# Gated linear attention: gate logits on four row strips of TensorE, scans by head between the tiles, the output gate projected early, and a per-token norm from 64 columns

## The reference, cut to what matters

```python
q = (x @ Wq).reshape(B, T, 4, 128);  k = (x @ Wk).reshape(B, T, 4, 128);  v = (x @ Wv).reshape(B, T, 4, 32)
gk = jax.nn.log_sigmoid(x @ Wgk1 @ Wgk2 + bgk2) / 16.0        # Wgk1 128x16, Wgk2 16x512: 4 heads x 128
# in chunks of 64 tokens: G = cumsum(gk) within the chunk
qg = q * exp(G) * scale;  k_intra = k * exp(-G);  kg = k * exp(G[last] - G)
o = tril(qg @ k_intra.T) @ v + qg @ S;   S = S * exp(G[last]) + kg.T @ v
g = (x @ Wg).reshape(B, T, 4, 32)
o = o * rsqrt(mean(o * o, axis=-1) + EPS) * gnw               # mean over the 32 values of a head
out = (o * silu(g)).reshape(B, T, 128) @ Wo
```

## Time and profile before

| | |
|---|---|
| median of 3 timed runs | 1602.13 us |
| lowest, highest | 1594.62, 1602.46 us |
| span of the profiled execution | 1577.7 us |
| from that span to the median of the runs | 24.4 us |
| busy in the span | PE 1150.9, DVE 839.3, ACT 752.6, POOL 533.3 us |

### The profile page before, as it was taken

How to read it: one execution, slowest core, us unless ns; L and a number is a source line. 1 busy time by engine, 2 the same in 40 slices (tenths; PEclk the granted TensorE clock), 3 DMA queues, 4 the chain that set the end, 5 groups by cost and what they waited for, 6 DMA issues and landing times. The chain is left out here.

```text
span 1577.7 us, 20354 instructions
## 1 busy us (share of the span) xinstructions
PE 1150.9 (73%) x6768; PEld 804.0 (51%) x6768; DVE 839.3 (53%) x1759; ACT 752.6 (48%) x1801; POOL 533.3 (34%) x532
## 2 busy tenths in 40 slices
PE   6639958996999676367686776876777748287897
PEld 2138825672666222255564555655555536174554
DVE  2075555534553566466665665656556546034536
ACT  4722336771875544255444454445445434074425
POOL 2000000000000448366666666666666653600000
PEclk8559978995999566576656767667666555578999
DMA  5000000000003235112222122222222212200000
GB/s 181 0 1 0 0 0 0 1 0 0 1 1 87 76 90 139 46 32 56 54 54 56 32 56 54 57 55 47 41 57 55 54 25 41 57 5 27 1 1 27
DMA packets 74367, 61.82 MB, mean 39 GB/s; under 512 B 31570, under 2 KB 58900, under 8 KB 73764
## 3 DMA queue, kind: packets, MB, share of 16 engines
q1 hardware_dynamic: 58404, 36.28, 9.3%
q0 software_dynamic: 15872, 24.41, 6.7%
HBM read 52.51 MB, written 8.13 MB: 38 GB/s over the span
## 5 line engine op out<-in xcount | busy, mean ns | idle before, releaser
L542 POOL DMA_INDIRECT arena_lo<-key_table,idx_T x496 | 491.9, 992 | 304.0 <-issue 134.8
L576 PE MATMUL bank<-arena_lo 128*32 128x32 f32 (+6 forms) x1656 | 208.5, 276 | 116.1 <-ACT arena_hi L1280 66.6
L576 PEld LDWEIGHTS bank<-arena_lo 128*32 128x32 f32 (+5 forms) x1656 | 177.7, 166 | 168.4 <-issue 131.2
L555 POOL TENSOR_TENSOR arena_lo<-arena_lo 128x512 f32<-128x512 f32 x8 | 11.8, 1474 | 516.4 <-DVE arena_lo L1608 516.1
L856 PE MATMUL bank<-ident,arena_hi 128*96 128x128 f32 x512 | 113.4, 363 | 24.4 <-DVE arena_hi L1700 23.2
L1254 ACT ACTIVATE arena_hi<-bank 96x512 f32<-96x512 f32 x128 | 74.7, 583 | 113.6 <-remote 67.3
L1280 ACT ACTIVATE arena_hi<-bank 32x128 f32<-32x128 f32 x128 | 33.5, 262 | 194.0 <-remote 160.7
L1668 DVE SCALAR_TENSOR_TENSOR arena_lo<-arena_lo,iw 128x512 f32<-128x512 f32 (+4 forms) x114 | 76.1, 668 | 81.5 <-ACT arena_lo L1237 46.2
L1237 ACT ACTIVATE arena_lo<-bank 128x512 f32<-128x512 f32 (+4 forms) x152 | 76.5, 512 | 65.7 <-remote 30.9
L576 PE MATMUL bank<-index_k_hi,index_q 128*128 128x512 f32 (+5 forms) x160 | 94.0, 589 | 18.7 <-issue 17.0
L1710 DVE CUSTOM_DVE_ANT_0 arena_hi<-bank,score_mask 128x208 f32<-128x208 f32 x124 | 46.4, 374 | 106.9 <-issue 71.0
(11 more groups left out here) (257 smaller groups left out, 2484.3 us busy)
## 6 DMA issues: line engine op xcount, KB each, us to landing
arena_lo<-key_table,idx_T POOLq DMA_INDIRECT x496
arena_lo<-q_l SPq DMA_DIRECT2D x64, 64.0 KB
arena_lo<-q_lat SPq DMA_DIRECT2D x32, 128.0 KB
arena_lo<-q_g SPq DMA_DIRECT2D x64, 64.0 KB
h<-in_h SPq DMA_DIRECT2D x2, 1024.0 KB, 8.2
q_l<-arena_hi SPq DMA_DIRECT2D x8, 256.0 KB
q_g<-arena_hi SPq DMA_DIRECT2D x8, 256.0 KB
q_lat<-arena_hi SPq DMA_DIRECT2D x8, 256.0 KB
```

Source lines behind the costliest of these rows:

```text
L542: pool.indirect_dma_start(out=G[b][:, q, :], out_offset=None, in_=key_table[0:index_width(i), :], in_offset=bass.IndirectOffsetOnAxis(ap=i ...
L576: return pe.matmul(out_, lhsT, rhs, start=start, stop=stop, **kw)
```

## The change

- The logits: `Wgk1` and `Wgk2` come from the host laid out anew. `Wgk1` is 128x128, its 16 columns repeated at the rows 0, 32, 64 and 96 of the product, the other columns zero; `Wgk2` is 128x128 with head `h`'s piece in the rows `32h` to `32h+15`. The four heads' matmuls then each use one strip of 32 rows of the array (`tile_position`) and a bank of their own. ACT does `Abs` alone; DVE reads the bank after it and writes the negated logit (`g_lin`). The next chunk's 16 values are projected and copied before this chunk's `Exp`.
- The sums: one head of one chunk at a time (`cumulate(k)`), rectifying in the same instruction as the addition. Five are done before the tiles, the other eleven one behind each of the tiles 0 to 10. ACT's `Exp` of a tile waits only for its own chunk.
- The output gate is projected into the banks 4 to 7 and taken through `Silu` before the first tile, into a buffer of its own (`gate`, named `arena_hi`).
- The tiles: the loops are written out. DVE no longer copies a tile of `xn` (`stage`, L1459); PE reads `xn` itself. ACT squares the tile's result out of `bank[3]` behind the tile, PE multiplies that 128x128 square with `head_mean` (128x4) to 4 columns of `bank[6]`, with the tokens on the partitions, and DVE's copy out of `bank[3]` becomes a product with `gnw` and the gate, behind ACT's square.
- The norm: ACT takes the root of the 128x64 columns, DVE the reciprocal, ACT spreads each column over 32 (`o_cols`), PE transposes them back to the layout of `oT`, DVE multiplies, PE projects with `gWo`, and DVE adds to `x`, chunk by chunk.
- Some buffers move, and `Wgk1`, `Wgk2` are 64 KB each in place of 8 and 32 KB; `mean_head` (64 KB) gives way to `head_mean` (2 KB).

```diff
-                with pe.Fori(0, NCH) as c:
+                def lowrank(c):
                     pe.wait_ge(ln_applied, LN0 + 4 * L_GLA + 1 + c)
-                    pe.wait_ge(g_rect, GH * c + 1)
-                    mm(bank[0][0:16, :], Wgk1[:], chunk(xn, c)).then_inc(g_r, 1)
+                    if c >= 1:
+                        pe.wait_ge(g_lin, GH * (c - 1) + 1)
+                    mm(bank[0], Wgk1[:], chunk(xn, c)).then_inc(g_r, 1)
+                def logits(c):
+                    strip = P // GH
                     pe.wait_ge(g_rs, c + 1)
                     for h in range(GH):
-                        pe.wait_ge(g_rect, GH * c + h + 1)
-                        mm(bank[h], Wgk2[:, h * GDK:(h + 1) * GDK], r_sb).then_inc(g_z, 1)
-                pe.wait_ge(g_rect, GH * NCH + GH)
+                        if c >= 1:
+                            pe.wait_ge(g_lin, GH * (c - 1) + h + 1)
+                        rows_ = slice(h * strip, (h + 1) * strip)
+                        mm(bank[h], Wgk2[rows_, :], r_sb[rows_, :], tile_position=(h * strip, 0)).then_inc(g_z, 1)
+                lowrank(0)
+                for c in range(NCH):
+                    logits(c)
+                    if c + 1 < NCH:
+                        lowrank(c + 1)
+                for c in range(NCH):
+                    mm(bank[4 + c], gWg[:], chunk(xn, c)).then_inc(g_gp, 1)
+                pe.wait_ge(g_lin, GH * NCH)
...
+                def mean_square(i):
+                    pe.wait_ge(g_osq, i + 1)
+                    mm(bank[6][:, 2 * P + GH * i:2 * P + GH * (i + 1)], o_sq, head_mean[:], skip_group_check=True)\
+                        .then_inc(g_oms, 1)
...
                     pe.wait_ge(g_S, 2 * i + 1)
+                    if not first:
+                        mean_square(i - 1)
...
                 project(0, "keys", first=True)
                 project(0, "queries", first=True)
+                pe.wait_ge(g_gate, NCH)
                 tile(0, 0, first=True)
-                with pe.Fori(0, NT // 2 - 1) as r:
-                    for u in (1, 0):
-                        tile(2 * r + 2 - u, u)
+                for i in range(1, NT - 1):
+                    tile(i, i % 2)
                 tile(NT - 1, 1, last_tile=True)
-                with pe.Fori(0, 2) as r:
-                    for u in range(2):
-                        c = 2 * r + u
-                        pe.wait_ge(g_gate, c + 1)
-                        mm(bank[u], gWg[:], chunk(xn, c)).then_inc(g_gp, 1)
-                with pe.Fori(0, 2) as r:
-                    for u in range(2):
-                        pe.wait_ge(g_osq, 2 * r + u + 1)
-                        mm(bank[2 + u], mean_head[:], o_sq[:, u, :]).then_inc(g_oms, 1)
-                    for u in range(2):
-                        pe.wait_ge(g_on, 2 * r + u + 1)
-                        mm(bank[u], gWo[:], chunk(oT, 2 * r + u)).then_inc(g_y, 1)
+                pe.wait_ge(g_S, 2 * NT + 1)
+                mean_square(NT - 1)
+                pe.wait_ge(g_qk, 2 * NT)
+                pe.wait_ge(g_vts, NT)
+                pe.wait_ge(g_out, NT)
+                pe.wait_ge(g_osq, NT)
+                def project_out(c):
+                    pe.wait_ge(g_on, c + 1)
+                    if c >= 2:
+                        pe.wait_ge(x_ready, 4 * L_FFN0 + c - 1)
+                    mm(bank[2 + c % 2], gWo[:], chunk(oT, c)).then_inc(g_y, 1)
+                for c in range(NCH):
+                    pe.wait_ge(g_oc, NCH + c + 1)
+                    if c >= 2:
+                        pe.wait_ge(g_on, c - 1)
+                    for j in range(C // P):
+                        last = pe.transpose(bank[c % 2][:, j * P:(j + 1) * P],
+                                            o_cols[c % 2][:, GH * j:GH * (j + 1), :].rearrange("p a b -> p (a b)"), ident[:])
+                    last.then_inc(g_ort, 1)
+                    if c >= 1:
+                        project_out(c - 1)
+                project_out(NCH - 1)
...
-                act.wait_ge(g_nb, 1)
+                def lowrank(c):
+                    act.wait_ge(g_r, c + 1)
+                    if c >= 1:
+                        act.wait_ge(g_z, GH * c)
+                    fn(r_sb, bank[0], ACT.Copy).then_inc(g_rs, 1)
+                lowrank(0)
                 for c in range(NCH):
-                    act.wait_ge(g_r, c + 1)
-                    fn(r_sb, bank[0][0:16, :], ACT.Copy).then_inc(g_rs, 1)
                     for h in range(GH):
                         act.wait_ge(g_z, GH * c + h + 1)
-                        fn(chunk(G_all[:, h, :], c), bank[h], ACT.Abs, bias=bgk2[:, h:h + 1])
-                        fn(chunk(relu_z[:, h, :], c), bank[h], ACT.Relu, scale=-1.0, bias=neg_bgk2[:, h:h + 1])\
-                            .then_inc(g_rect, 1)
-                    act.wait_ge(g_rect, GH * (c + 2))
+                        fn(chunk(G_all[:, h, :], c), bank[h], ACT.Abs, bias=bgk2[:, h:h + 1]).then_inc(g_rect, 1)
+                    if c + 1 < NCH:
+                        lowrank(c + 1)
+                    act.wait_ge(g_rect, GH * (c + 1))
                     g = G_all[:, :, bass.ds(c * C, C)]
                     steps.did(fn(g, g, ACT.Exp, scale=-1.0))
                 steps.leave(NCH, 1)
                 for c in range(NCH):
                     g = G_all[:, :, bass.ds(c * C, C)]
                     fn(g, g, ACT.Ln, bias=one_col).then_inc(g_ln, 1)
+                for c in range(NCH):
+                    act.wait_ge(g_gp, c + 1)
+                    fn(chunk(gate, c), bank[4 + c], ACT.Silu).then_inc(g_gate, 1)
 
                 def prepare(n, u, first=False):
 
                     if not first:
                         act.wait_ge(g_S, 2 * n - 1)
                         act.wait_ge(g_qk, 2 * n - 1)
-                    act.wait_ge(g_G, NT)
+                    act.wait_ge(g_G, GH * (n * P // C + 1))
...
+                def square(i):
+                    act.wait_ge(g_o, i + 1)
+                    if i >= 1:
+                        act.wait_ge(g_oms, i)
+                    fn(o_sq, bank[3][:, 0:P], ACT.Square).then_inc(g_osq, 1)
                 def tile(i, u, first=False, last_tile=False):
+                    if not first:
+                        square(i - 1)
...
+                square(NT - 1)
+                act.wait_ge(g_oms, NT)
+                fn(o_sd, bank[6][:, 2 * P:2 * P + NT * GH], ACT.Sqrt, bias=eps_col).then_inc(g_osd, 1)
+                act.wait_ge(g_osd, 2)
                 for c in range(NCH):
-                    act.wait_ge(g_gp, c + 1)
-                    fn(chunk(gate, c), bank[c % 2], ACT.Silu).then_inc(g_gate, 1)
-                act.wait_ge(g_out, NT)
-                with act.Fori(0, 2) as r:
-                    for u in range(2):
-                        fn(o_sq[:, u, :], chunk(oT, 2 * r + u), ACT.Square).then_inc(g_osq, 1)
-                    for u in range(2):
-                        act.wait_ge(g_oms, 2 * r + u + 1)
-                        fn(o_sd[:, u, :], bank[2 + u], ACT.Sqrt, bias=eps_col).then_inc(g_osd, 1)
+                    if c >= 2:
+                        act.wait_ge(g_ort, NCH + c - 1)
+                    per = GH * C // P
+                    fn(o_cols[c % 2], o_sd[:, per * c:per * (c + 1)].unsqueeze(2).to_broadcast([P, per, GDV]), ACT.Copy)\
+                        .then_inc(g_oc, 1)
...
-                with dve.Fori(0, NCH) as c:
-                    steps.enter(c, 1)
+                for c in range(NCH):
+                    for h in range(GH):
+                        dve.wait_ge(g_rect, GH * c + h + 1)
+                        if c == 0 and h == 0:
+                            dve.wait_ge(g_nb, 1)
+                        v.tensor_scalar(chunk(relu_z[:, h, :], c), bank[h], -1.0, neg_bgk2[:, h:h + 1], ALU.mult, ALU.add)\
+                            .then_inc(g_lin, 1)
+                def cumulate(k):
+                    c, h = k // GH, k % GH
                     dve.wait_ge(g_ln, c + 1)
-                    g, z = (a[:, :, bass.ds(c * C, C)] for a in (G_all, relu_z))
-                    steps.did(v.tensor_tensor(z, z, g, ALU.add))
-                    for h in range(GH):
-                        last = v.tensor_tensor_scan(chunk(G_all[:, h, :], c), scan_keep[:], chunk(relu_z[:, h, :], c),
-                                                    0.0, ALU.mult, ALU.add)
-                    last.then_inc(g_G, C // P)
-                steps.leave(1, NCH)
+                    dve.wait_ge(g_lin, k + 1)
+                    g, z = (chunk(a[:, h, :], c) for a in (G_all, relu_z))
+                    steps.did(v.scalar_tensor_tensor(z, z, 0.0, g, ALU.max, ALU.add))
+                    v.tensor_tensor_scan(g, scan_keep[:], z, 0.0, ALU.mult, ALU.add).then_inc(g_G, 1)
+                for k in range(GH + 1):
+                    cumulate(k)
...
                 def read_out(n):
-                    dve.wait_ge(g_o, n + 1)
```

(50 more changed lines are left out.)

49 lines of the change are left out of this document (26 added, 23 removed).

## The result

The changed kernel takes 1534.2 us (median of 4 runs, 1523.6 to 1544.0) against 1598.4 us before (4 runs, 1589.3 to 1602.5): a ratio of 0.962, 95% interval 0.954 to 0.969. Forecast were 1547 us, within 1534 to 1562. The profiled execution took 1542.15 us with a span of 1540.3. Some executions run slower as a whole at a lower granted clock: the medians in this text are over all executions, the ratios and intervals leave those out, so that a ratio can differ a little from the quotient of two medians.

A forecast was written before the change was run, and what follows sets the result against it. Engines were taken to wait on each other in turn, with PE bounding only the tiles. Gains 37.6 + 0 - 3.6 - 5.2 + 25.0 = 53.8, plus 1.2, made 55; 1602.1 - 55 = 1547 us, range 1534 to 1562.

The forecast's parts named there:

- Logits, 5.9 us a chunk, last Exp at 51.9: Logits stage: four heads side by side in 1.71 us, 5.9 us from Exp to Exp; gain 21.3 us.
- the strips' rival: Logits: strips don't run side by side, 6.8 us a chunk, 15 us lost, 1562 us; chance 0.08.
- that of the written order: Logits: passes start in written order, 4.3 us a chunk, 1552 us in all; chance 0.08.
- The 1.2 us added for the logits' clock: Logits: PE's clock perhaps up in part with four strips at work; 1.2 us more gain.
- First tile's Exp at 66.5: Between logits and tiles: ACT's Ln, Silu and table loads set the first Exp, 66.5 against 104.1; gain so far 37.6 us.
- First tile, even: First tile: projections already made but PE longer at half clock; 11.3 us from Exp to second tile as before, gain 0.
- Tiles, +8.8: Tiles: mean's matmul adds 0.24 us a tile, 3.6 in all; late scans add 1.74 us three times, 5.2.
- 2.63 us idle didn't lower the clock: Tiles: PE's earlier 2.63 us idle left the clock up, an argument against it falling at pauses of 1.74 us.
- The rival of the falling clock: Tiles: half clock makes each about 5.9 us longer, slower kernel from 10 tiles on, 1641 us with all 16; chance 0.02.
- Norm and output, 15.5 us: From the last tile's start to the next layer's first matmul: 15.5 us against 40.5; gain 25.0, bounds 20 and 26.3.
- The layer norm behind it, unchanged: Layer norm behind the output projection: left unchanged, no gain or loss counted.
- The median of the runs lies 24.4 above the span.: Whole kernel, from profiled span to run time: span 1577.7 us, median of the runs 1602.1 before the change.

The follow-up runs named there:

- the copy: after run again, unchanged; this time no GpSimd cast held up DVE's products in the first layer norm: 1372.7 us against 1423.7 before, ratio 0.966.
- after: The changed kernel as described, against the kernel before: 1534.2 us against 1598.4, ratio 0.962.
- its own experiment: The changed kernel with all four heads' logits weights on one strip of rows 0 to 31, one behind another: 1378.7 us, ratio 0.966 to before.
- the idle matmuls: The changed kernel with 14 matmuls that nobody reads on PE ahead of the first tile: 1553.8 us, ratio 0.967 to before.
- the other two groups: Unchanged repeats of before and after, each pair on one chip: 1423.7 and 1372.7 us, ratio 0.966; 1417.9 and 1360.4 us, ratio 0.960.

## Why the prediction was right, and where not

Set beside the copy of after without the collision (the forecast knew only a layer norm without it), the layer went from 222.6 to 170.3 us, and the stretch behind it from 28.7 to 26.3: 54.7 us, where 55 were forecast. With the collision on both sides (225.6 and 175.0, the stretch behind 29.5 and 27.7) it is 52.4. That the sum comes so near is in part luck: its terms missed in both directions, and two of the signs that the prediction itself named for being wrong did show. The clock was below 1.0 between the second tile and the last (0.95 over the 14 tiles), and tiles without a chunk's edge took over 6.6 us (7.39 and 6.98, the ones behind a long tile). Term by term:

- **Logits, 5.9 us a chunk, last Exp at 51.9.** The last Exp ended at 51.5 in the copy (58.0 in after, behind the collision), so the gain of 21.3 holds. But the period is 6.5: I let the Exp (1.91) cover the logits (1.71), and with 2.09 for them and 0.65 and 0.4 of hand-over they are what ACT waits for. The first chunk, at full clock (1.14 us for eight records), was earlier than I had it and made up for it. On the factor: 2.09 us against 7.19 is 3.4 times, between the 4 that I took and the 3.07 of the Trainium skill (TensorE: Matmul & The Clock Gate, Part 3), and the 2.2 us by that rule was the nearer. The two groups of four starts are as forecast: the strips' rival and that of the written order are refuted, the first by its own experiment. The 1.2 us added for the logits' clock has no row of its own: granted were 0.69 in the copy in place of 0.54, and the last Exp came 0.4 earlier than forecast.
- **First tile's Exp at 66.5.** 65.2 in the copy. ACT set it, as said; 1.84 us for a sum and scan, with 1.95 taken. The terms that the prediction names add up to 65.8, not 66.5 (51.9 and 1.28, 7.68, 1.28, 2.36, 1.28), so that 0.7 us of the miss is in the sum.
- **First tile, even.** 10.2 us in after against 11.26, 1.1 better, mostly at half clock (0.66 granted on the mean). What the full clock gives was shown by the idle matmuls: 2.3 us in one pair of profiles, 2.4 in the other.
- **Tiles, +8.8.** They cost 10.6 in after and 11.9 in the copy. The mean's matmul costs 0.12 a tile and not 0.24 (6.21 against 6.09), 1.7 us in all. The late scan costs 1.60 each, with 1.74 forecast, three times. The step that failed is the clock: "2.63 us idle didn't lower the clock" was carried from a place behind the tiles to one inside them. There shorter pauses, of 1.33 us (the tile grows by 1.60), were followed by half clock in two of three cases in after and in all three in the copy; that is 4.1 and 5.4 us. The rival of the falling clock was real, at a tenth of the size at which it would decide. That DVE has room for a scan in a tile held; it waits 0.67 us for PE in one.
- **Norm and output, 15.5 us.** 16.3 in after, 15.8 in the copy. Right, with part of it at half clock, as between the two bounds given.
- **The layer norm behind it, unchanged.** It is 1.0 us shorter in after and 2.4 in the copy, where the clock was at 1.00 throughout; before, its granted clock was 0.90, with its beginning at half (four `x,center` matmuls in 3.13 us, in after 1.88). This I had left out.
- **"The median of the runs lies 24.4 above the span."** This step is wrong. After's profiled execution took 1542.15 us with a span of 1540.3, 1.8 more, and so did each of its four runs (1523.56 with 1521.8). The runs of before in the other groups lie 1.8 to 3.3 above their spans, so its profiled execution took about 1579.5 to 1581 us, some 20 less than the runs' median: inferred, for that time isn't listed. It did no harm, since in the end 55 were taken from 1602. Of the 12.8 us between forecast and result, 3.7 are the lower median of before with its fourth run, and 9 the wider difference of 64 us; the other two groups had 51 and 57.6, so I take these 9 for the scatter of the untouched stages, not for a gain of the change. That 1534.2 still lies within the stated 1534 to 1562 is luck of this scatter, for it lies at the very edge. What makes these stages vary, and differ by some 170 us between chips, wasn't tried.

## What to carry to other kernels

Where work moves from ahead of a loop into its turns, look at the turn in which it is first needed: there one piece more ahead of the loop cost nothing and gave back the 9 us that the late pieces took. A buffer that is reused for something small (bank 0 for 16 rows) can be the circle that sets a stage's pace when its big users have become fast. And with untouched stages that scatter by 10 us, a change of 50 is read by the length of its own layer, between two marks that both kernels have, and only held against the times.

## What the runs showed of the hardware

- Four fp32 matmuls of 32 rows on four row strips, two passes each: all first passes start within 0.02 us, all second ones 1.0 us behind. They take 2.09 us in all at half clock, against 7.19 one behind another, and 1.14 at full clock.
- A DVE product of two SBUF operands (128x512, 0.69 us) takes 2.0 to 2.3 us when a GpSimd cast of 128x2048 (1.90 alone) started 0.2 to 0.7 us ahead of it. It was so in the kernel before, too: 5 of the 10 profiles in which nothing kept them apart have it. The cast waits for a transfer and the product for the norm, and which comes first differs from execution to execution. Where such a cast starts behind it, the product takes 0.9 at most.
- The same pause of PE, 1.33 us inside an otherwise busy stretch, came 21 times in seven profiles with late scans. In 17 cases half clock was granted behind it, for 3.4 or 6.8 us, in 4 it wasn't; what sets these apart isn't shown. In the four profiles without the pause (one scan more ahead in three of them, all scans ahead in one) the clock was 1.00 through all of the tiles 1 to 14.
